# Packing the edge counts of a graph kernel in eight three-bit digits instead of six four-bit ones

## The reference

```
src, dst: (16384,) int32, in 0..511, sorted by dst
h = relu(layernorm(x))
q, k, v = h @ Wq + bq, h @ Wk + bk, h @ Wv + bv              # 512 x 512 each
scores = einsum('nhd,mhd->nhm', q, k) / 8
adj = zeros((512, 512)).at[src, dst].set(1.0)
attn = softmax(where(adj == 0, -1e9, scores), axis=1)
...
aggr = segment_sum(h[src], dst)                              # later layers: sums over edges
```

## Time and profile before

| | us |
|---|---|
| median of 3 runs | 519.67 |
| lowest, highest | 519.45, 520.11 |
| the profiled execution's own time | 517.47 |
| its span, first to last instruction | 515.7 |

### The profile page before, as it was taken

One profiled execution on the slowest core, in us unless ns is written; L12 is line 12 of the kernel. 1 busy time (PEld: TensorE's weight loads), 2 busy tenths in 40 slices (PEclk: granted clock), 3 DMA queues, 4 the chain that ended last, 5 costly groups with the idle time before them and its releaser, 6 DMA issues.

```text
span 515.7 us, 6318 instructions
## 1 busy us (share of the span) xinstructions
PE 462.6 (90%) x2235; PEld 341.5 (66%) x2235; DVE 319.4 (62%) x630; ACT 202.5 (39%) x258; POOL 155.5 (30%) x100
## 2 busy tenths in 40 slices
PE   3999899688887899969979999999999999999794
PEld 2467444233344787847858888888888888888582
DVE  5999982899995888594496224622362336232846
ACT  4989833545413242135162224123413341333223
POOL 3000000011011696429360433443344334433100
PEclk9899999999988999989998999999999999999898
DMA  8840000000011123302201024202420332010002
GB/s 255 242 168 0 2 2 20 1 0 1 1 51 51 42 81 123 147 16 104 81 10 74 0 90 135 102 1 107 159 83 5 133 128 81 10 72 1 0 1 82
DMA packets 22476, 34.36 MB, mean 67 GB/s; under 512 B 5680, under 2 KB 5936, under 8 KB 22448
## 3 DMA queue, kind: packets, MB, share of 16 engines
q1 hardware_dynamic: 22160, 33.85, 19.4%
q10 hardware_dynamic: 288, 0.13, 0.1%
HBM read 32.93 MB, written 1.05 MB: 66 GB/s over the span
## 4 chain that ended last, share of the span: by engine, by line
PE 60%; DVE 21%; ACT 9%; issue 5%; POOL 4%; DMA 1%; ACTq 0%; SPq 0%; DVEq 0%
PE ps L1106 15%; PE ps L1107 15%; PE ps L1108 15%; PE ps L1170 4%; ACT distance L541 3%; DVE rsum L867 3%; PE ps L1134 3%; PE ps L1135 3%; PE ps L1177 2%; ACT one_dst L546 2%; DVE e_sb L365 2%; DVE stats L684 2%; DVE half_sum L863 2%; POOL x_sb L469 1%; PE ps L1119 1%
## 5 line engine op out<-in xcount | busy, mean ns | idle before, releaser
L444 POOL TENSOR_TENSOR w_lo<-w_stage,w_hi 128x1024 fp32r<-128x1024 f32 x22 | 52.7, 2393 | 137.6 <-ACT w_hi L511 137.6
L511 ACT ACTIVATE w_hi<-w_stage 128x2048 fp32r<-128x2048 f32 x23 | 43.9, 1909 | 73.0 <-PE ps L1108 73.0
L445 POOL TENSOR_TENSOR w_lo<-w_stage,w_hi 128x1024 fp32r<-128x1024 f32 x22 | 57.4, 2607 | 0.0
L1107 PE MATMUL ps<-w_lo,hid_hi 128*128 128x512 f32 x128 | 49.9, 390 | 0.0
L1106 PE MATMUL ps<-w_hi,hid_hi 128*128 128x512 f32 x128 | 49.9, 390 | 0.0
L1108 PE MATMUL ps<-w_hi,hid_lo 128*128 128x512 f32 x128 | 49.9, 390 | 0.0
L1039 DVE TENSOR_SCALAR tmp<-ps,bl 128x512 f32<-128x512 f32 x16 | 12.0, 751 | 52.1 <-ACT hid_hi L646 52.1
L1106 PE MATMUL ps<-T_hi,w_hi 128*128 128x512 f32 (+1 forms) x112 | 41.5, 371 | 1.8 <-DVE T_lo L713 1.4
L1107 PE MATMUL ps<-T_lo,w_hi 128*128 128x512 f32 (+1 forms) x112 | 41.0, 366 | 0.0
L1108 PE MATMUL ps<-T_hi,w_lo 128*128 128x512 f32 (+1 forms) x112 | 40.9, 365 | 0.0
L453 POOL TENSOR_TENSOR w_lo<-w_stage,w_hi 128x512 fp32r<-128x512 f32 x4 | 5.1, 1264 | 106.2 <-DVE rsum L865 106.2
(11 more groups left out here) (188 smaller groups left out, 1094.6 us busy)
## 6 DMA issues: line engine op xcount, KB each, us to landing
w_stage<-in_L_gnn_Wr SPq DMA_DIRECT2D x8, 1024.0 KB, 5.2
w_stage<-in_L_gnn_Wl SPq DMA_DIRECT2D x8, 1024.0 KB, 5.2
w_stage<-in_L_gnn_W SPq DMA_DIRECT2D x5, 1024.0 KB, 6.3
x_sb<-in_x SPq DMA_DIRECT2D x4, 256.0 KB, 3.7
w_q<-in_L_gnn_Wq SPq DMA_DIRECT2D x1, 1024.0 KB, 7.5
w_k<-in_L_gnn_Wk SPq DMA_DIRECT2D x1, 1024.0 KB, 9.9
w_v<-in_L_gnn_Wv SPq DMA_DIRECT2D x1, 1024.0 KB, 5.6
w_o<-in_L_gnn_Wo SPq DMA_DIRECT2D x1, 1024.0 KB, 8.7
```

The costliest lines, as they stand in the source:

```text
L444: gp.tensor_tensor(w_lo[s][:, 0:2], stage[s][:, 0:2], f32(w_hi[s][:, 0:2]), ALU.subtract)
L445: gp.tensor_tensor(w_lo[s][:, 2:4], stage[s][:, 2:4], f32(w_hi[s][:, 2:4]), ALU.subtract)\
L511: nc.scalar.activation(w_hi[u % 2][:], stage[u % 2][:], ACT.Copy).then_inc(hi_made, 1)
L1107: nc.tensor.matmul(goal, a_hi, b_lo, start=False, stop=False, **kw)
```

## The change

A number in PSUM now holds eight digits of three bits: four quarters of the destinations by two halves of the sources. `one_dst` shrinks from 128x256 to 128x128, `one_src` grows from 128x172 to 128x256, and a chunk takes one matmul instead of two. VectorE makes its four `one_dst` of a group in one instruction, which compares `iota_n`, repeated for each chunk, with `inner_dst`, each of whose numbers is repeated along 128 columns. The preparation of the digits goes by integer masks and shifts, and the weight is written as the exponent bits of a float. Both remaining copies of `T_sb` and the four of k move from VectorE to ScalarE, `neg_ident` moves behind the making of `no_edge`, TensorE's pattern of groups becomes 1, 1, 2, 2 and 2, 2, 3, 3, and its wait for k moves behind the read of the flag. The float copy `edge_f` of the edges is made in the slow branch only.

More of the change, by code:

```diff
@@ L127, in build @@
     edge_f = place("edge_f", [P, 2, CH], F32, rEP + MAT + 1024)
-    upper = place("upper", [P, 2, CH], F32, rEP + MAT + 2048)
+    part_no = place("part_no", [P, 2, CH], I32, rEP + MAT + 1024)
+    inner = place("inner", [P, 2, CH], I32, rEP + MAT + 2048)
     edge_m = place("edge_m", [P, 2, CH], F32, rEP + MAT + 3072)
@@ L131, in build @@
     iota_n = place("iota_n", [P, N], F16, rEP + MAT + 4608)
-    packed = place("packed", [P, 2, THIRD], I32, rEP + MAT + 5632)
-    distance = place("distance", [P, ACT_CHUNKS, HALF], F16, rEP + 2 * MAT)
-    edge_neg = place("edge_neg", [P, CH], F32, rEP + 2 * MAT + 2048)
+    packed = place("packed", [P, HALF], I32, rEP + MAT + 5632)
+    inner_dst = place("inner_dst", [P, CH], F16, rEP + MAT + 6656)
     checked = place("checked", [P, 2], F32, rEP + MAT + 7680)
     slow_flag = place("slow_flag", [P, 1], I32, rEP + MAT + 7712)
+    distance = place("distance", [P, ACT_CHUNKS, P], F16, rEP + 2 * MAT)
     zeros = place("zeros", [P, N], F16, rEP)
@@ L271, in build @@
         ct_ready = sem("ct_ready")
-        T_made = [sem("T_made_act"), sem("T_made_dve")]
+        T_made = sem("T_made")
+        edges_whole = sem("edges_whole")
         sums_made, rinv_made = sem("sums_made"), sem("rinv_made")
@@ L547, in packed_one_hots @@
                                          bias=one_col).then_inc(onehot_act, 1)
-            for t in (0, 2):
+            for t in range(NT):
                 act.wait_ge(tr_done, tr_no(T0, t))
                 nc.scalar.activation(T_sb[:, :, t * P:(t + 1) * P], ps[:, t, :].rearrange("p (k n) -> p k n", k=DT),
-                                     ACT.Copy).then_inc(T_made[0], 1)
+                                     ACT.Copy).then_inc(T_made, 1)
             act.wait_ge(consts, 4)
@@ L725, in _ @@
             v.wait_ge(edges_in, 32)
[L726 to L731, removed]
-                                                ALU.mult, ALU.add))
@@ L733, in _ @@
[L733 to L740, removed]
@@ L770, in _ @@
             packed_one_hots(3 * RING, RING)
-            v.wait_ge(cols_in, 16 * (5 + EXPERTS))
-            for j in range(PAIRS):
-                v.wait_ge(k_done, j + 1)
-                nc.vector.tensor_scalar(k_sb[:, j, :], ps[:, k_bank(j), :], bk[:, j:j + 1], None, ALU.add)\
-                  .then_inc(k_made, 1)
-            v.wait_ge(onehot_used, CH // UN)
-            counted = ps[:, 7, 0:2 * THIRD]
-            link(nc.vector.tensor_scalar(packed[:], counted.rearrange("p (m n) -> p m n", m=2), W_SCALE, 2.0 ** 24,
-                                         ALU.mult, ALU.min))
-            for src_up in range(3):
-                width = min(THIRD, N - src_up * THIRD)
-                for dst_up in range(2):
-                    shift_by = DIGIT * (dst_up + 2 * src_up)
-                    last = nc.vector.tensor_scalar(
-                        digits[:, 2 * dst_up:2 * dst_up + 2, src_up * THIRD:src_up * THIRD + width],
-                        packed[:, :, 0:width], shift_by,
-                        2 ** DIGIT - 1 if shift_by < 5 * DIGIT else 2 ** 24 - 1, ALU.logical_shift_right,
-                        ALU.bitwise_and)
+            v.wait_ge(onehot_used, CH // UN)
+            counted = ps[:, 7, 0:HALF]
[5 more added lines that the diff above has]
+                                               ALU.logical_shift_right, ALU.bitwise_and)
             last.then_inc(digits_made, 1)
@@ L813, in whole_one_hots @@
                                             ALU.is_equal).then_inc(all_onehot, 1)
+                nc.vector.tensor_copy(edge_f[:], edge_i[:]).then_inc(edges_whole, 1)
+                v.wait_ge(edges_whole, 1)
                 for s in range(UW):
```

10 lines of the change are left out of this document (2 added, 8 removed).

## The result

| | before | after |
|---|---|---|
| median, first comparison | 519.56 (4 runs) | 505.59 (4 runs) |
| the profiled execution's own time | 517.47 | 505.41 |
| its span | 515.7 | 503.6 |

The ratio of the first comparison is 0.9733, with a 95% interval from 0.9714 to 0.9752: 13.97 us faster, where 10.9 was forecast (508.8) and the range began at 505.5. So the time lies 0.1 us inside the range, and outside the gain of 9.5 to 12.5 us to which the forecast itself gave 0.62. The spans of the two traces differ by 12.1 us only. In two later comparisons the same changed kernel had ratios of 0.9777 (0.9736 to 0.9818) and 0.9735 (0.9700 to 0.9769). By the medians, the gain is 12 to 14 us; the experiments say why it is not known more closely.

A forecast was written before the change was run, and what follows sets the result against it. Three nearly level engines were taken to bound the count stage ahead of the scores. The count ending 10.6 us earlier plus 0.3 for k's wait gave 10.9, so 519.67 - 10.9 = 508.8 us, range 505.5 to 514.5.

The forecast's parts named there:

- The start: Ahead of the counts: ScalarE's four T_sb copies end at about 12.3, TensorE starts at 12.4, VectorE's first one-hots at 11.9.
- VectorE's turn: VectorE's count loop: one comparison and eight one_src take 2.7 us a turn instead of 3.31, about covering the end's idle time.
- The first rival: VectorE's loop keeps 0.28 us idle: 3.05 a turn, gain 5.9, time 513.8; chance 0.20, shared with dearer one_src.
- the slow rival: VectorE's widened one_src costs 1.04 ns a column and never runs ahead: 3.53 us a turn, 521.5 us; chance 0.03.
- The broadcast comparison: VectorE's comparison over 512 columns: taken at the upper 0.69 us, 0.60 to the next start; the lower row was 0.425.
- ScalarE's turn: ScalarE's count loop: 2.3 us a turn instead of 3.14, or 2.6 if register instructions hold the distances at 0.4 spacing.
- 8.80 + 20.8 + 14.1: TensorE's count stage: first two tiles, other tiles and groups of 0.88 sum to 43.7 us from 12.4, ending at 56.1.
- a rival with a chance of 0.11: TensorE's first tiles run at full clock, 1.9 us to spare; VectorE alone ends the count at 56.1: 508.1 us.
- The sum of the stage: Count stage: last count ends at 56.7, 10.6 us earlier, and k's wait gives 0.3 more.
- ScalarE's allowance: End of the count: 56.1 with ScalarE's turn at 2.3 us, 57.6 at 2.6; 56.7 was taken.
- The tail: VectorE's work behind the count stays hidden: 1.6 us of cover against about 0.4 more work; scores 10.86 us after 56.8.
- Gain carried to the median: Whole time: the scores' 10.9 us gain subtracted from the median, 519.67 - 10.9 = 508.8.

The follow-up runs named there:

- the four comparisons: Changed kernel with VectorE's one broadcast comparison of a group taken apart into four of 128 columns: 514.55 us, ratio 0.9913 to the kernel before.
- The moves alone: Kernel before with old digits and one-hots; T_sb and k copies on ScalarE, k's wait behind the flag, neg_ident late: 516.33 against 518.25, ratio 0.9961.

## Why the prediction was right, point by point

The mechanism was right and the stage's gain close: 10.9 us for the start of the scores, 12.4 in the first trace. That the time fell into the range is partly luck. The stage alone gives 507.5, and the other 1.9 us, by which it came within 0.1 us of the range's end, are scatter of the two sets of runs as far as the record shows.

- **The start.** ScalarE's four copies ended at 12.15 and TensorE began at 12.19 (12.3 and 12.4 forecast), VectorE at 11.95 (11.9). Right; both move by 0.6 from trace to trace.
- **VectorE's turn.** 2.7 was taken, 2.66 measured, with the comparison at 0.68 (0.69) and `one_src` at 0.334 (0.355). The first rival, that the loop's end shows, is refuted by the missing idle time, and the four comparisons show the mechanism from the other side. The 84 more columns cost 9 ns by the mean durations (325 and 334), but those move with what runs beside them: with one comparison and 172 columns the mean was 395. From start to start, eight `one_src` took 2.06 us at 256 columns and 1.87 at 172, so 24 ns each, about the 30 taken; the slow rival needed 90.
- **The broadcast comparison.** It took 678 ns for 512 columns, as the 4-byte row had it (692) and not the plain 16-bit row (425). The next instruction started 0.60 us behind it, and 1.14 behind the one of 1024 columns: 1.05 ns a column. The Trainium skill (Vector Engine (DVE) Microarchitecture Reference, section 5.1) has a two-source operation on 2-byte operands, one of them one element read again and again, at one element a cycle. This case's traces agree.
- **ScalarE's turn.** 2.3 was taken as likely and 2.6 as the other bound; it was 2.28. The 0.6 us that I put on the end of the count for the dearer bound was not needed.
- **TensorE.** A group of 0.87 (0.88). The step that was mis-sized is "8.80 + 20.8 + 14.1": it kept the 8.80 of two half-pace tiles in the forecast and put the full pace in a rival with a chance of 0.11. The two tiles took 7.9 from start to start without the group between them (6.9 is full pace), and 3.70 for the first one in the two later traces, which is that rival. In all three traces TensorE waited at the end for VectorE. That rival's sum, an end at 56.1 by VectorE alone, was the nearest to the measured 55.4.
- **The sum of the stage.** v tiles at 55.42 where 56.8 was forecast: 0.6 of the 1.4 is ScalarE's allowance and 0.7 VectorE's sixteen turns at 2.654 on average instead of 2.7. The quicker tiles had to come too, since TensorE's own sum also stood at 56.1.
- **The tail.** The scores came 10.6 us behind the first v tile (10.9 forecast, 10.7 in the timeline of the kernel before), with `ct_ready` at 64.68 and so 1.4 us to spare. Right; the wait for k was gone.
- **Gain carried to the median.** "I carry the gain over: 519.67 - 10.9". The traces' 12.1 taken from the 519.56 of the comparison gives 507.5; 505.59 was measured, and 1.9 us lie in no stage of the two traces. The median that I subtracted from was high: the same kernel later had 518.25, 517.98 and 517.97. I had treated three runs within 0.7 us as the kernel's whole scatter, and "0.2% is what a measurement can tell" was too fine: single executions go over 6 us.

## What to carry to other kernels

Where short instructions are addressed by loop registers, count instructions before columns: four compares of 128 columns made a turn of 3.28 us and one of 512 made it 2.66, mostly because the long one covers the register work of the loop. Where several engines are level, price every one of them. The moves alone brought the v tiles 2.1 us forward; the one comparison on top of them added nothing, the new digits on top of them 1.0 (1.8 at the full clock), and both together 10.2. A stall at the head of an engine that ends up waiting for another costs nothing up to the length of that wait (here 0.5 to 1.5 us), so a forecast should add it only after asking who ends the stage.

## What the hardware showed that I had not expected

- At the start of a program the granted clock read 1.00 while matmuls ran at half pace (0.85 us apart against 0.43, 9.17 us for two tiles against 7.13). Full pace came with the first entry of the clock in the trace, anywhere from 10.1 to 20.2 us over the fourteen traces.
- The spots where the clock falls are not the same from one execution of one kernel to the next. The times of the kernel before went over 6 us (514.99 to 520.91), while its two traces differ by 0.4 us in the stage studied.
- 84 more columns of a 16-bit comparison against a column operand cost about 24 ns from start to start. A second column operand, with the second operation that uses it, cost more than that: 334 ns for 256 columns with two operands, 285 with one, by mean durations.
